# Waiting for a chunk's indirect transfers before the next chunk's are issued, in the routing and the gather loop of a two-block metaformer kernel

## What is computed

```python
x = x + _L0_conv_ref(_ln_c(x), ...)        # three table-lookup convolutions (softmax over 16 centroids)
t = _to_tokens(x)                          # 32 * 196 = 6272 tokens of 256 numbers
t = t + _L0_ffn_ref(_ln_t(t), router_w, expert_weights)
x = _from_tokens(t, x)
x = x + _L1_conv_ref(_ln_c(x), ...)        # a gated squeeze-and-excite scaling
t = _to_tokens(x)
t = t + _L1_ffn_ref(_ln_t(t), ...)         # per-head experts, top 2 of 16
```

```python
rw = softmax(logits).reshape(T, E)
vals, idx = jax.lax.top_k(rw, TOP_K)                         # TOP_K = 2
w_masked = zeros_like(rw).at[arange(T)[:, None], idx].set(vals)
# out = sum over experts e of (x_flat * w_masked[:, e]) @ W_e
```

## Time and profile before

| | us |
|---|---|
| median of 3 timed runs | 2380.0 (2377.4 to 2391.9) |
| span of the profiled execution | 2466.2 |
| of it: before the routing stage | 713 |
| routing stage | 283 |
| expert stage | 176 |
| gather stage | 383 |
| last stage | 911 |

### The profile page before, as it was taken

How to read it: one execution, slowest core, us unless ns; L and a number is a source line. 1 busy time by engine, 2 the same in 40 slices (tenths; PEclk the granted TensorE clock), 3 DMA queues, 4 the chain that set the end, 5 groups by cost and what they waited for, 6 DMA issues and landing times. The chain is left out here.

```text
span 2466.2 us, 36023 instructions
## 1 busy us (share of the span) xinstructions
PE 2088.2 (85%) x12850; PEld 1155.0 (47%) x12851; DVE 1331.5 (54%) x2117; ACT 1290.4 (52%) x1634; POOL 818.1 (33%) x608
## 2 busy tenths in 40 slices
PE   6998699997975653788289887799999999999998
PEld 3444355554544442577155554344444444444443
DVE  5666435554555554122166675366666766666633
ACT  2444222222542221122134342698989989988997
POOL 4332211120005554000657511234434334334343
PEclk8999779998996665899578896899999999999999
DMA  2010211212523331576323311555565655556554
GB/s 54 27 34 8 85 59 59 69 55 85 198 89 107 104 100 43 161 209 198 95 64 114 105 59 60 143 162 158 163 162 153 163 155 159 159 160 163 155 151 117
DMA packets 280563, 281.24 MB, mean 114 GB/s; under 512 B 44998, under 2 KB 261654, under 8 KB 280278
## 3 DMA queue, kind: packets, MB, share of 16 engines
q1 hardware_dynamic: 246422, 233.49, 33.8%
q0 software_dynamic: 12288, 25.72, 3.5%
q10 hardware_dynamic: 21696, 19.93, 2.4%
HBM read 203.76 MB, written 75.25 MB: 113 GB/s over the span
## 5 line engine op out<-in xcount | busy, mean ns | idle before, releaser
L2326 ACT ACTIVATE BIG<-psA,b_s 128x1024 f32<-128x1024 f32 x784 | 809.8, 1116 | 89.8 <-PE psA L2265 82.2
L2254 POOL TENSOR_TENSOR BIG<-BIG 128x1024 f32<-128x1024 f32 x147 | 359.6, 2446 | 553.1 <-DVE BIG L2347 553.1
L2265 PE MATMUL psA<-x_r,w_r 128*128 128x512 f32 x1568 | 480.4, 427 | 20.4 <-DMA x_r<-hs_d 12.2
L2347 DVE SCALAR_TENSOR_TENSOR BIG<-psY,b_s,BIG 128x512 f32<-128x512 f32 x392 | 291.6, 749 | 247.6 <-PE psY L2275 246.8
L2265 PEld LDWEIGHTS psA<-x_r,w_r 128*128 128x128 f32 x1568 | 269.0, 190 | 330.5 <-ACT BIG L2326 244.9
L2275 PE MATMUL psY<-BIG,w_s 128*32 128x512 f32 x3136 | 400.9, 602 | 2.9 <-DVE BIG L2347 2.2
L1199 POOL DMA_INDIRECT xg_d<-xnb,SLOT x128 | 131.6, 1028 | 144.2 <-issue 75.4
L719 DVE TENSOR_REDUCE b_nm<-psN 112x32 f32<-112x512 f32 x128 | 83.1, 686 | 148.3 <-PE psN L616 147.8
L1774 POOL DMA_INDIRECT gath<-yg_d,SLOT x128 | 129.9, 1015 | 83.8 <-issue 42.9
L2275 PEld LDWEIGHTS psY<-BIG,w_s 128*32 128x32 f32 x3136 | 73.6, 108 | 160.9 <-issue 91.3
L719 DVE TENSOR_REDUCE a_nm<-psN 98x32 f32<-98x512 f32 x128 | 82.3, 685 | 90.8 <-PE psN L607 90.6
(11 more groups left out here) (394 smaller groups left out, 3242.9 us busy)
## 6 DMA issues: line engine op xcount, KB each, us to landing
BIG<-wt_d SPq DMA_DIRECT2D x784, 128.0 KB, 3.2
x_r<-hs_d SPq DMA_DIRECT2D x196, 128.0 KB, 3.5
xg_d<-ex SPq DMA_DIRECT2D x64, 264.0 KB, 3.6
xv<-xg_d SPq DMA_DIRECT2D x66, 256.0 KB, 3.1
BIG<-ypad_d SPq DMA_DIRECT2D x140, 120.0 KB
xv<-x SPq DMA_DIRECT2D x64, 196.0 KB, 2.6
hs_d<-xv SPq DMA_DIRECT2D x32, 392.0 KB
yg_d<-ex ACTq DMA_DIRECT2D x33, 256.0 KB, 3.6
```

The costliest lines, as they stand in the source:

```text
L2254: eng.tensor_tensor(gacc[:, w % 2], gacc[:, w % 2], gsum[:, a % 2], ALU.add).then_inc(Q["acc"], 1)
L2265: mm = eng.matmul(psA[m % 3][:, b * BLK:(b + 1) * BLK], w1_r[:, m % 16], x_r[:, w % 2, b * BLK:(b + 1) * BLK], start=True, stop=True)
L2326: eng.activation(hid[:, m % 8], psA[m % 3][:], ACT.Gelu, bias=b1_s[:, m % 16:m % 16 + 1]).then_inc(Q["gel"], 1)
L2347: eng.scalar_tensor_tensor(out=dst, in0=psY[use % 2][:], scalar=b2_s[:, g % 4:g % 4 + 1], in1=wb[:, g % 3, b * BLK:(b + 1) * BLK], op0=ALU ...
```

## The change

Ahead of the eight indirect DMAs of a chunk, GpSimd now also waits until the eight of the chunk before have landed; in the routing loop on `d_sc` of that chunk's buffer, in the gather loop on `h_g`. The first chunk has no such wait, so there are fifteen in each loop. Nothing else differs.

```diff
@@ -1194,6 +1194,8 @@
                 for t in range(T):
                     wait(eng, D["slot"], t // GC + 1)
                     wait(eng, D["ev"], 2 * (t + 1))
+                    if t > 0:
+                        wait(eng, d_sc[(t - 1) % XB], ((t - 1) // XB + 1) * 16 * NSUB * 2)
                     for s in range(NSUB):
                         for j in range(2):
                             eng.indirect_dma_start(
@@ -1769,6 +1771,8 @@
                 def gather(c):
                     wait(eng, H["w0"], c - GB + 1)
                     wait(eng, H["y"], 2 * (c - GB + 1))
+                    if c > 0:
+                        wait(eng, h_g[(c - 1) % GB], ((c - 1) // GB + 1) * 16 * NSUB * 2)
                     for s in range(NSUB):
                         for j in range(2):
                             eng.indirect_dma_start(gath[:, c % GB, 2 * s + j], None, yg_d.ap(),
```

## The result

| | us |
|---|---|
| before, median | 2382.6 |
| after, median | 2412.7 |
| ratio, with its 95% interval | 1.013 (1.010 to 1.016) |
| span of the profiled execution after | 2411.8 |

The changed kernel is slower by 1.3%, about 31 us (24 to 38). 2398 us had been forecast, 2355 to 2418 as the range. This time the span of the profiled execution and the timed runs agree.

A forecast was written before the change was run, and what follows sets the result against it. GpSimd, without slack beside the chain making SLOT, was taken to bound the routing loop; 19 us there plus 3 in the gather loop made 22, lowered to 18: 2380 + 18 = 2398 us, range 2355 to 2418.

The forecast's parts named there:

- The time that the sum was made against: Whole kernel: timed median 2380.0 us, not the profiled span of 2466.2 us, taken as the ground for the added price.
- the 78 us of holds: Routing and gather stages: late TensorE signals during GpSimd's bursts, 78.3 us, inferred to occur only in the execution being recorded.
- Rival A: L1249, L1278, L1806, L1810: timed runs have the holds too and the pauses end them; about 2324 us; chance 0.2.
- The price of one wait: GpSimd at a chunk boundary, both loops: landing behind the issue costs 1.4 us a wait, ends 1.0 and 1.95.
- its own sign: Gap between scatters of successive chunks: 1.3 to 2.3 us expected; under or over that, the price is wrong.
- The Trainium skill's 2.0 us: Fixed cost of each GpSimd DMA; less the 0.3 us gap, 15 x 1.7 = 25.5 us in the routing loop.
- Routing loop: Scatters: GpSimd has no slack, so 15 x 1.4 = 21 us less about 2 reach the barrier: 19 us.
- slack that timed runs might give GpSimd: Whole sum: timed runs may give GpSimd somewhat more slack than the recorded one, so 18 us taken instead of 22.
- the ring: Routing loop, XB=5 buffers: lateness does not stop the chain; chunk 10's buffer 14 us late, 21 us left.
- Gather loop: Gathers: from chunk 5 waits hide under VectorE's `yn`, gaps unchanged; only the ramp pays, 3 us (0 to 6).
- Rival B: Both loops: every landing costs the upper price, 29 + 6 = 35 us, 2415 us; chance 0.12.
- More than 1% slower: Whole kernel, over 2404 us: rival B, half of rival D and the upper part of the own case; chance 0.28.

## Why the prediction was wrong, by its steps

**The time that the sum was made against: right.** 2380 us was the right ground and the 78 us of holds were no part of the kernel: recorded again, it has a span of 2388.0 us and no hold. The reason was drawn too widely, though. The prediction said that holds belong to the execution that is being recorded; the recordings of four kernels here whose routing loop is that of before (before itself, the waits in the gather loop after eight, and both after four) have none there. It was one odd execution. No run here shows whether the path that the Trainium skill describes in "NOTIFIC — the notification-queue block", section 7.1, had a part in it. What raised the holds in that one execution stays open.

**Rival A: fell, and its test was weak.** L1249 lost its "remote" waits and the span fell by 54 us, to 2411.8, as the text foresaw. That looked like pauses that end the holds. The kernel before without holds shows that they go without pauses too; only the timed median, which rose, spoke on A.

**The price of one wait: this is the step that failed.** 1.4 us was taken, with 1.95 as the upper end; it is 2.38 - 0.30 = 2.08 us. The landing itself was read well enough: 2.5 to 2.6 us from the start of an issue in the median, less its 0.96, is 1.5 to 1.6 us. What was missing is GpSimd's start behind it. The prediction took 0.3 us for that from a SLOT; at the boundary of a chunk it is 0.85 us. The 0.3 us hold for a landing too where GpSimd awaits nothing else: in the middle of a chunk (waits after every four scatters) it starts 0.29 us behind it, and such a wait costs 1.76 - 0.30 = 1.46 us, nearly the 1.4 forecast. What the prediction left out is that its wait joins two others, for SLOT and the evacuation, and the 0.56 us that the start takes longer there. It also took ScalarE's start behind the gathers for GpSimd's. By its own sign, a gap over 2.3 us, the price was wrong.
The Trainium skill's 2.0 us ("DMA: Bandwidth & Descriptors", "Anatomy of one DMA — SWDGE (gpsimd) path"), less the usual gap, were nearer, an estimate of 1.7 us against 2.08 measured. The 25.5 us made of them stand against 15 x 2.08 = 31.2 us of gaps, and come near the loop's 26.3 only because some 5 us of the gaps are given back.

**Routing loop: the mechanism right, the size off by the price.** GpSimd had no slack worth naming, and the rise goes through the barrier undiminished. The gaps sum to 36.3 us, against 7.9 in the kernel before (twelve of 0.30, two of 1.51, one of 1.29, the last three being waits for SLOT): 28.4 more, of which the shorter bursts give back 2.1. So 26.3 us where 19 were forecast; with 2.08 in the place of 1.4 the forecast's own sum, 15 x 2.08 less 2 and less the 3.4 us of SLOT waits that it did not see, is 25.8. A second, smaller miss lies behind the sum: 22 us were lowered to 18 for slack that timed runs might give GpSimd, and no run shows any beyond those 3.4 us. The claim that the ring does not stop the chain was a little off: ScalarE waits for it four times, 16.0 us, because chunk 10 is 10 x 2.1 = 21 us late, which is just what the ring had left. It did no harm; the pace of SLOT stayed.

**Gather loop: 3 us forecast, 2.4 us measured (-2 to 7).** The reason given was only half right. The gaps from chunk 5 on were to stay unchanged, under waits for VectorE's `yn`. In the kernel before without holds GpSimd issues the gathers of chunks 0 to 8 without a stop, so the waits do lengthen the gaps ahead of chunks 5 to 8, and GpSimd falls behind. What hides them there is that it runs ahead: by chunk 8 its gathers are 27 us ahead of their reader (15 with the waits), and from there on the landing passes under `split`. The first chunks do pay, 8.0 us at chunk 4, but by the end of the loop nothing of it can be told from the spread of the recordings. The earlier trace rows came from a recording whose gather loop had been held up, and showed a cover that began too early. That has a limit: with waits after every four gathers the lateness reaches ScalarE by another way, through `split`, which the prediction named as queued behind the waits and did not price.

**The sum.** 26 us in the routing loop and 2 in the gather loop (not clear of nothing) make 28 of the 31 measured (24 to 38). Rival B, the upper price, came nearest: 2415 us forecast, 2413 measured. Its price was near (1.95 us a wait against 2.08), but its 29 us for the routing loop were 26 and its 6 for the gather loop 2, so that the sum is this close is in part luck. Its chance of 0.12 was too small, since the only rows that showed an engine released by such a landing gave 1.4 and 1.95. More than 1% slower, which came, had been given 0.28, less than within 1% with 0.55.

## What to carry to other kernels

A wait for one's own last transfer costs the whole latency behind its issue and the start of the issuing engine, as soon as that engine has no slack: here 1.5 us where the wait stood alone, and 2.1 us where it joined two others. Awaiting one transfer less took 1.2 us of it away, awaiting a whole chunk earlier took all. Price a wait with the waiting engine's own start, and at the place where it will stand, with the waits beside it. And where a recording is much longer than the timed runs, record again before reading slack and cover from it.

## What the runs showed of the hardware

How soon GpSimd resumes behind a landing hangs on what else it awaits there. In the kernel with waits in the gather loop alone, the boundary ahead of chunk 2, the one ahead of chunk 3, and ScalarE, released by the same landing as the second:

```profile
1138.62 0.97 POOL L1776 DMA_INDIRECT gath<-yg_d,SLOT  x1 [0.30 <-issue]
1141.55 0.97 POOL L1776 DMA_INDIRECT gath<-yg_d,SLOT  x1 [1.96 <-DMA gath<-yg_d,SLOT]
...
1150.60 0.96 POOL L1776 DMA_INDIRECT gath<-yg_d,SLOT  x1 [0.30 <-issue]
1154.07 0.97 POOL L1776 DMA_INDIRECT gath<-yg_d,SLOT  x1 [2.50 <-DMA gath<-yg_d,SLOT]
```
```profile
1153.24 1.70 ACT L1915 ACTIVATE yn<-gath,P 98x256 f32<-98x256 f32 x4 [5.21 <-DMA gath<-yg_d,SLOT]
```

The last gather of chunk 2 ends at 1151.57 us; ScalarE starts 1.67 us later, GpSimd 2.50. Ahead of chunk 2 GpSimd takes 1.96 us: there it awaits the landing alone, since its waits for ScalarE and VectorE begin with chunk 3 (`c - GB + 1` is not above 0 before). By the semaphores' times in the trace it starts 0.28 us behind the landing ahead of chunk 2, and 0.85 ahead of chunk 3, the two values of the routing loop with waits after every four scatters. Behind a SLOT it is 0.30 us. Ahead of chunk 3 the landing is awaited by the separate instruction (L48); its wait is over when ScalarE starts, at 1153.24 us, and 0.83 us lie from there to the gather. Why these pass, and whether it is the number of the waits or their order that brings them on, the runs don't show.
